# A vision tower with routed experts: GpSimd's wait for a scatter, and the place of a one-hot table

## The chip, the cores and the metric

The kernel runs on one core of one Trainium2 chip. The metric is device time in microseconds (us), the median of several executions. Before the change it was 946.81 us (three runs, 944.99 to 950.73).

## The reference, cut to what matters

The input is 32 images of 3 x 128 x 128. A tokenizer makes 64 tokens of 192 features of each, then follow a feed-forward layer, windowed attention and another feed-forward layer, a class token is put ahead (65 tokens an image, 2080 rows), then attention that keeps the 26 largest scores, and last the part that the change touches, a mixture of 128 experts:

```
topk_idx = top_k(sigmoid(x @ Wg.T) + e_bias, 6)      # 6 of 128 experts for each of 2080 rows
xb   = x[token_buf].reshape(E, CAP, H)               # up to 192 rows for each expert
gu   = einsum('ech,ehf->ecf', xb, W_gate_up);  g, u = split(gu, 2)
yb   = einsum('eci,eih->ech', silu(g) * u, W_down) * w_buf
out  = h + zeros.at[token_buf].add(yb) + silu(x @ Wsg) * (x @ Wsu) @ Wsd
```

Only experts that some row chose need work; with these inputs the experts' loop makes 20 rounds.

## The kernel before, in words

Five engines run programs of their own and meet at semaphores. Up to the experts the work goes over 16 tiles of 128 tokens; tables of words (`ORDER`) set by hand in which order each engine takes the pieces of neighbouring tiles. The normalized rows go to `x_rows` in DRAM, and what is not of the routed experts to `out`. The change touches none of these tables.

Then comes the experts' loop, `Fori(0, n2)`, each pass of which is two rounds (s = 0 and 1), one for each expert, on buffers that alternate. What a round v does:

- **SP** loads an expert's weights, two rounds ahead.
- **PE** makes the up products of half 0 (L996, L1001), then the index products (`slots_of`, L927) of expert v+2, which wait for `hot_ready`; then the up products of half 1, the transposes of the gathered rows of expert v+1 (L935), and the down products (L1012) of half 0 and, when DVE has them, of half 1.
- **ACT** makes the tanh of each half (L1191), copies the transposed rows (L1121), and scales the result into `y` (L1196, `y_done`).
- **DVE** finishes half 0 (L1628, L1632), waits for `add_done`, keeps the scatter's indices and weights (L1636, L1637), turns PE's index products into indices (L1551 to L1557, `index_ready`), then reads the number of the expert v+3 from a list (L1537, a register load) and builds a one-hot table of which row has which slot: a small part of 6 tiles (L1541, 1152 wide), after half 1 (L1628, L1632) a large part of 11 tiles (L1541, 2112 wide), and a copy of the weights (L1544), which signals `hot_ready`.
- **GpSimd** (POOL) issues the two gathers of expert v+2 once their indices are there (L1758), then waits for `y_done`, issues the two scatters that add y to `out` in DRAM (L1788), waits until they have landed (L1790), and signals `add_done`.

Indices that stand for no row point at dummy rows from T = 2080 on, of `x_rows` and of `out`. SP zeroes these with two transfers at the end of its first loads (L610, L611).

Of the kernel before, what the change touches and what calls it, by code (L numbers as in the profile page):

```python
# [6 lines left out]
D = 192  # L7
NP = (IMG // PATCH) ** 2
NKEY = NP + 1
T = B * NKEY  # L10
# [24 lines left out]
ROWS = T + CAP  # L35
# [271 lines left out]
def every(*stages):  # L307
# [4 lines left out]
SEMAPHORES = """  # L312
    h3_kept0 h3_kept1 xT_kept0 xT_kept1 fetched0 fetched1 at0_T at1_T at0_aT at1_aT zero_rows x_stored
    acc_stored0 acc_stored1 patch_mm xm_ready acc_ready c_xm_ready cls_x_stored  cls_acc_stored list_ready
# [16 lines left out]
def tower_kernel(nc, a, out):  # L331
# [4 lines left out]
    with ctx:  # L336
# [60 lines left out]
        zrows = sb("zrows", [CAP // 2, 2 * DX])  # L397
# [141 lines left out]
        def S(name):  # L539
            return named[name]  # L540
# [61 lines left out]
        def _(sp):  # L602
            sp.dma_start(xp[:], a["xp"][0]).then_inc(xp_loaded, 16)
            for group, done in ((patch_loads, loads_patch), (tokenizer_loads, loads_tokenizer),
# [3 lines left out]
                for dst, src in group:  # L608
                    sp.dma_start(dst, src).then_inc(done, 16)
            sp.dma_start(x_rows[T:ROWS, :].rearrange("(p r) d -> p (r d)", r=2), zrows[:]).then_inc(S("zero_rows"), 16)  # L610
            sp.dma_start(out[T:ROWS, :].rearrange("(p r) d -> p (r d)", r=2), zrows[:, 0:2 * D]).then_inc(S("zero_rows"), 16)  # L611

# [588 lines left out]
        def _(dve):  # L1201
# [419 lines left out]
            with dve.Fori(0, n2) as i:  # L1621
                for s in range(2):
                    v = 2 * i + s + 1
                    slots = slots_of(2 * i + s + 3, 1 - s)
                    for r in range(2):
# [8 lines left out]
                        if r == 0:  # L1634
# [4 lines left out]
                            indices_of(s, v + 2)  # L1639
                        if r == 0:  # L1640
                            next(slots)
                    run(slots)
# [3 lines left out]
        def _(pool):  # L1646
            G = nc.gpsimd
# [113 lines left out]
            def gathers():  # L1761
                yield "gather0"
                pool.wait_ge(S("x_stored"), 64 * TILES + 64)
                pool.wait_ge(S("cls_x_stored"), 32)
                pool.wait_ge(S("zero_rows"), 32)
                gather(0, 1)
                yield "gather1"
                gather(1, 2)

            pool.wait_ge(S("pe_ready"), 1)  # L1770
            pool.wait_ge(loads_tokenizer, 16 * len(tokenizer_loads))
# [4 lines left out]
            n2 = pool.value_load(lists[0:1, 2 * LIST:2 * LIST + 1], min_val=1, max_val=E // 2)  # L1776
            pool.sem_inc(S("add_done"), 2)
            for s in range(2):
                pool.wait_ge(S(f"acc_stored{s}"), 16 * TILES)
            pool.wait_ge(S("cls_acc_stored"), 16)  # L1780
            with pool.Fori(0, n2) as i:
                for s in range(2):
                    v = 2 * i + s + 1
                    gather(s, v + 2)
                    hold(pool, S("y_done"), v + 2)

                    for h in range(2):
                        G.indirect_dma_start(out[:, :], bass.IndirectOffsetOnAxis(add_index[s][:, h:h + 1], 0),  # L1788
                                             y[s][:, h, :], None, compute_op=ALU.add).then_inc(S("added"), 16)
                    pool.wait_ge(S("added"), 64 * i + 32 * s + 32)  # L1790
                    pool.sem_inc(S("add_done"), 1)
            for s in range(2):
# [78 lines left out]
```

## Time and profile before

| | us |
|---|---|
| median of three runs | 946.81 |
| the profiled execution, its own time | 954.78 |
| its span, first to last instruction | 953.0 |
| PE busy | 846.6 (89%) |
| DVE busy | 750.6 (79%) |
| ACT busy | 343.4 (36%) |
| POOL busy | 308.2 (32%) |

The profile cuts the span into 40 slices, lists who waited for whom, follows the chain of work that ended last back from the end, and gives each engine's instructions in order of time. The tiles take the first 700 us, the experts' loop the last 220. TensorE's granted clock was 0.965 over the whole, 0.97 in the loop. DMA engines are busy for about half of the loop's time.

### The profile page before, as it was taken

The page shows a single profiled execution, that of the slowest core. Times are in us where ns is not written, and L with a number is a line of the kernel's source. Part 1 is how long each engine was busy: PE and PEld are TensorE (multiplying, and loading weights), DVE is VectorE, ACT ScalarE, POOL GpSimd, SP SyncE. Part 2 cuts the span into 40 slices and gives each one's busy share as a digit, 9 for nine tenths or more (in the row PEclk, how much of TensorE's full clock was granted, in tenths as well). Part 3 has the DMA queues.
Part 4 walks back from the last instruction along what each step waited for, and adds up shares of the span by engine and source line. Part 5 has one row for each costly group of instructions (what it writes and reads, how often), then busy time and mean ns, then how long its engine had stood idle before and what let it go on. Part 6 is the DMA issues. An engine that isn't in the chain of part 4 may idle for free.

```text
span 953.0 us, 22207 instructions
## 1 busy us (share of the span) xinstructions
PE 846.6 (89%) x7603; PEld 766.5 (80%) x7603; DVE 750.6 (79%) x3738; ACT 343.4 (36%) x971; POOL 308.2 (32%) x350
## 2 busy tenths in 40 slices
PE   1787899899899899899899999998999999999993
PEld 1676688788798788788799999988878878878782
DVE  4256899999899899899999896988635666676662
ACT  0325554553553554544544435331100222122220
POOL 6021212412412312312313311031102556656564
PEclk8799999999999999999999999999986999999997
DMA  7410010110001001001101000001104455565541
GB/s 204 127 51 1 2 35 16 37 32 21 29 20 33 29 17 35 30 17 35 29 19 35 26 20 27 25 25 41 45 5 112 115 143 147 128 152 142 128 115 29
DMA packets 48663, 54.25 MB, mean 57 GB/s; under 512 B 8981, under 2 KB 41595, under 8 KB 48540
## 3 DMA queue, kind: packets, MB, share of 16 engines
q1 hardware_dynamic: 39372, 44.23, 16.3%
q0 software_dynamic: 6592, 7.28, 4.8%
q10 hardware_dynamic: 2608, 1.60, 0.7%
q8 instruction: 48, 0.79, 0.3%
q14 instruction: 43, 0.35, 0.1%
HBM read 42.40 MB, written 10.69 MB: 56 GB/s over the span
## 4 chain that ended last, share of the span: by engine, by line
DVE 41%; PE 28%; issue 11%; POOL 7%; DMA 7%; ACT 3%; SPq 2%; DVEq 0%; POOLq 0%; ACTq 0%
DVE b_arena L1497 10%; POOL b_arena L1758 4%; DMA out_rows<-b_hid,b_add_index 3%; POOL out_rows L1788 3%; DMA out_rows<-b_inner,b_add_index 3%; DVE b_top_a L1483 3%; PE p_big L685 3%; PE p_big L686 2%; DVE b_top_d L1483 2%; PE p_shared L830 2%; DVE b_top_c L1483 2%; PE p_shared L831 2%; DVE b_top_b L1483 2%; DVE b_rstd L1235 2%; PE p_small L866 2%
## 5 line engine op out<-in xcount | busy, mean ns | idle before, releaser
L1758 POOL DMA_INDIRECT b_arena<-x_rows,b_index x44 | 75.0, 1705 | 103.4 <-issue 66.3
L1541 DVE TENSOR_TENSOR b_arena<-b_iota_b,b_slot 128x1152 bf16<-128x1152 bf16 (+1 forms) x46 | 85.2, 1855 | 15.0 <-issue 15.0
L685 PE MATMUL p_big<-b_xT,b_ff1a 128*128 128x128 f32 x384 | 77.7, 285 | 1.4 <-ACT b_xT L1025 1.4
L686 PE MATMUL p_big<-b_xT,b_ff1b 128*128 128x128 f32 x384 | 76.9, 283 | 0.0
L1692 POOL TENSOR_TENSOR b_arena<-b_kY,b_mask_k 64x256 f32<-64x256 f32 x16 | 9.8, 611 | 204.8 <-ACT b_kY L1050 204.8
L1025 ACT COPY b_xT<-p_small 128x256 f32<-128x256 f32 (+1 forms) x97 | 35.5, 377 | 83.2 <-PE p_small L676 83.1
L1723 POOL TENSOR_TENSOR b_arena<-b_arena 128x768 f32<-128x768 f32 x16 | 27.0, 1690 | 117.6 <-DVE b_arena L1509 117.6
L685 PEld LDWEIGHTS p_big<-b_xT,b_ff1a 128*128 128x128 f32 x384 | 61.8, 200 | 2.5 <-ACT b_xT L1025 2.5
L686 PEld LDWEIGHTS p_big<-b_xT,b_ff1b 128*128 128x128 f32 x384 | 61.1, 200 | 0.0
L996 PE MATMUL p_big<-b_xeT,b_arena 128*116 128x192 f32 x320 | 60.1, 331 | 0.0
L719 PE MATMUL p_big<-b_arena,b_q_blk 128*128 128x256 f32 (+3 forms) x256 | 48.9, 334 | 12.4 <-ACT b_q_blk L1057 12.4
L719 PEld LDWEIGHTS p_big<-b_arena,b_q_blk 128*128 128x128 f32 x256 | 41.3, 190 | 19.3 <-POOL b_arena L1692 12.5
L996 PEld LDWEIGHTS p_big<-b_xeT,b_arena 128*116 128x116 f32 x320 | 51.5, 180 | 0.3 <-issue 0.3
L866 PE MATMUL p_small<-b_patch_w,b_xp 128*128 128x192 f32 x192 | 38.3, 353 | 11.8 <-DMA b_pe<-in_pe 9.9
L1107 ACT ACTIVATE b_th<-p_shared 116x256 f32<-116x256 f32 (+1 forms) x50 | 18.9, 377 | 71.5 <-PE p_shared L831 64.0
L866 PEld LDWEIGHTS p_small<-b_patch_w,b_xp 128*128 128x128 f32 x192 | 33.9, 205 | 13.2 <-issue 9.9
L1628 DVE SCALAR_TENSOR_TENSOR b_hid<-b_hid,p_big 116x384 f32<-116x384 f32 x20 | 11.1, 554 | 39.2 <-ACT b_hid L1191 39.2
L927 PEld LDWEIGHTS p_small<-b_rhs,b_arena 128*96 128x96 bf16 x748 | 37.0, 129 | 6.2 <-issue 4.7
L1497 DVE MATCH_REPLACE8 b_arena<-b_top_c,b_arena 128x65 f32<-128x65 f32 x208 | 41.7, 211 | 0.0
L836 PE MATMUL p_shared<-b_wsd,b_inner 116*128 116x192 f32 (+1 forms) x208 | 40.8, 354 | 0.9 <-DVE b_inner L1313 0.8
L1497 DVE MATCH_REPLACE8 b_arena<-b_top_b,b_arena 128x65 f32<-128x65 f32 x208 | 41.3, 211 | 0.0
L1497 DVE MATCH_REPLACE8 b_arena<-b_top_a,b_arena 128x65 f32<-128x65 f32 x208 | 41.1, 212 | 0.0
(367 smaller groups left out, 2589.6 us busy)
## 6 DMA issues: line engine op xcount, KB each, us to landing
b_arena<-in_w_gate_up SPq DMA_DIRECT2D x20, 464.0 KB
b_arena<-in_w_down SPq DMA_DIRECT2D x20, 336.0 KB
b_xp<-in_xp SPq DMA_DIRECT2D x16, 384.0 KB, 3.1
b_arena<-in_w_gate_up SPq DMA_DIRECT2D x40, 116.0 KB
xT_rows<-b_xmT SPq DMA_DIRECT2D x16, 128.0 KB, 1.8
b_xT_late<-xT_rows SPq DMA_DIRECT2D x16, 128.0 KB, 2.2
h_rows<-b_h SPq DMA_DIRECT2D x16, 96.0 KB, 1.6
x_rows<-b_xm SPq DMA_DIRECT2D x32, 48.0 KB, 2.0
```

The costliest lines, as they stand in the source:

```text
L685: mm(o, ff1a[:, c * 128:(c + 1) * 128], xTa[s][:], start=True, stop=False)
L686: last = mm(o, ff1b[:, c * 128:(c + 1) * 128], xTb[s][:], start=False, stop=True)
L719: last = mm(big[s][:, g, at:(4 + 2 * m) * keys], q_blk[s][:, m, g, :], k[:, g, :, :].rearrange("p j k -> p (j k)"), start=True, stop=True)
L836: last = mm(shared_bank(v, 4)[0:rows, 0:D], inner[:, c, 0:rows], wsd[:, c, :], start=(c == 0), stop=(c == NSC - 1))
L866: last = mm(small[2][:, 0:D], xp[:, c, :], patch_w[:, c, :], start=(c == 0), stop=(c == KC - 1))
L927: last = mm(lists_bank[s][0:HS, 400 + 6 * h:406 + 6 * h], hot[s][:, t, h * HS:(h + 1) * HS], rhs[s][:, t, :], start=(t == 0), stop=(t == N ...
L996: mm(big[r][0:SC, bank, j * CAP:(j + 1) * CAP], w_gu[s][:, c:c + SC], xeT[s][:, 0, :], start=(j == 0), stop=False)
L1025: cp((xT[s] if to is None else to)[:, 0:256].rearrange(both, t=128)[:, :, 0:rows], small[s][:, 0:256].rearrange(both, t=128)[:, :, 0:rows] ...
L1483: last = V.max(top[:, 8 * h:8 * h + 8], src[:, h * NKEY:(h + 1) * NKEY])
L1497: last = V.match_replace(work[:, h * NKEY:(h + 1) * NKEY], top[:, 8 * h:8 * h + 8], src[:, h * NKEY:(h + 1) * NKEY], -3e38)
L1541: last = tt(hot[s][:, tiles, :], iota_b[:, None, :].to_broadcast([128, n, CAP]), slot[:, tiles, bass.ds(e, 1)].to_broadcast([128, n, CAP]) ...
L1758: G.indirect_dma_start(xg[s][:, h, :], None, x_rows[:, :], bass.IndirectOffsetOnAxis(index[s][:, h:h + 1], 0)).then_inc(S(f"gathered{s}"), 16)
```

## The change

Three edits, with the bookkeeping of their semaphores:

1. GpSimd waits for a scatter's landing not behind its issue but just ahead of the next scatter's, and signals `add_done` there. `add_done` starts at 1 and not at 2, so DVE still reads it as "the scatter of round v-2 has landed".
2. DVE makes no part of the one-hot table between the halves. The register load, both parts and the copy stand behind half 1.
3. The two transfers of zero rows are issued by GpSimd behind its memsets. They count on the scatters' semaphore.

```diff
-            sp.dma_start(x_rows[T:ROWS, :].rearrange("(p r) d -> p (r d)", r=2), zrows[:]).then_inc(S("zero_rows"), 16)
-            sp.dma_start(out[T:ROWS, :].rearrange("(p r) d -> p (r d)", r=2), zrows[:, 0:2 * D]).then_inc(S("zero_rows"), 16)
...
                             indices_of(s, v + 2)
-                        if r == 0:
-                            next(slots)
                     run(slots)
...
-                pool.wait_ge(S("zero_rows"), 32)
+                pool.wait_ge(S("added"), 32)
                 gather(0, 1)
...
+            pool.wait_ge(presets, 1)
+            G.dma_start(x_rows[T:ROWS, :].rearrange("(p r) d -> p (r d)", r=2), zrows[:]).then_inc(S("added"), 16)
+            G.dma_start(out[T:ROWS, :].rearrange("(p r) d -> p (r d)", r=2), zrows[:, 0:2 * D]).then_inc(S("added"), 16)
             pool.wait_ge(S("pe_ready"), 1)
...
-            pool.sem_inc(S("add_done"), 2)
+            pool.sem_inc(S("add_done"), 1)
...
                     gather(s, v + 2)
                     hold(pool, S("y_done"), v + 2)
-
+                    hold(pool, S("added"), 64 * i + 32 * s + 32)
+                    pool.sem_inc(S("add_done"), 1)
                     for h in range(2):
                         G.indirect_dma_start(out[:, :], bass.IndirectOffsetOnAxis(add_index[s][:, h:h + 1], 0),
                                              y[s][:, h, :], None, compute_op=ALU.add).then_inc(S("added"), 16)
-                    pool.wait_ge(S("added"), 64 * i + 32 * s + 32)
-                    pool.sem_inc(S("add_done"), 1)
+            pool.wait_ge(S("added"), 64 * n2 + 32)
```

The order on DVE in a round of the loop, from the last index instruction to the end of the table, before (b_arena<-b_iota_b,b_slot is the one-hot table, b_rhs the copy of the weights; ISA rows are register work):

```order
1839 L1557 SCALAR_TENSOR_TENSOR b_index<-p_small,b_slot_a 96x2 [waits s_index_part]
1840 L1537 ISA
1841 L1537 TENSOR_LOAD b_lists
1842 L1537 ISA x2
1843 L1541 ISA
1844 L1541 TENSOR_TENSOR b_arena<-b_iota_b,b_slot 128x1152
1845 L1628 SCALAR_TENSOR_TENSOR b_inner<-b_inner,p_big 116x384 [waits s_eth1]
1846 L1632 TENSOR_TENSOR b_arena<-b_inner,p_big 116x384 [waits s_esilu]
1847 L1541 ISA
1848 L1541 TENSOR_TENSOR b_arena<-b_iota_b,b_slot 128x2112
1849 L1544 ISA
1850 L1544 COPY b_rhs<-b_wsplit 128x17x3
```

And with the change (its line numbers are lower by two):

```order
1839 L1555 SCALAR_TENSOR_TENSOR b_index<-p_small,b_slot_a 96x2 [waits s_index_part]
1840 L1626 SCALAR_TENSOR_TENSOR b_inner<-b_inner,p_big 116x384 [waits s_eth1]
1841 L1630 TENSOR_TENSOR b_arena<-b_inner,p_big 116x384 [waits s_esilu]
1842 L1535 ISA
1843 L1535 TENSOR_LOAD b_lists
1844 L1535 ISA x2
1845 L1539 ISA
1846 L1539 TENSOR_TENSOR b_arena<-b_iota_b,b_slot 128x1152
1847 L1539 ISA
1848 L1539 TENSOR_TENSOR b_arena<-b_iota_b,b_slot 128x2112
1849 L1542 ISA
1850 L1542 COPY b_rhs<-b_wsplit 128x17x3
```

The two instructions of half 1 moved ahead of the register load and of the small part.

On GpSimd, one round and the start of the next, before:

```order
277 L1758 DMA b_arena<-x_rows,b_index 96x256 [waits s_index_ready]
278 L1758 DMA b_arena<-x_rows,b_index 96x256
279 L1788 DMA out_rows<-b_hid,b_add_index 2272x192 [waits s_y_done]
280 L1788 DMA out_rows<-b_hid,b_add_index 2272x192
281 L1790 ISA
282 L544 REGISTER_ALU [waits s_added]
283 L1758 DMA b_arena<-x_rows,b_index 96x256 [waits s_index_ready]
```

And with the change:

```order
279 L1754 DMA b_arena<-x_rows,b_index 96x256 [waits s_index_ready]
280 L1754 DMA b_arena<-x_rows,b_index 96x256
281 L544 ISA [waits s_y_done]
282 L1788 DMA out_rows<-b_hid,b_add_index 2272x192 [waits s_added]
283 L1788 DMA out_rows<-b_hid,b_add_index 2272x192
284 L544 REGISTER_ALU
285 L1754 DMA b_arena<-x_rows,b_index 96x256 [waits s_index_ready]
```

The wait for the landed scatters no longer stands between a scatter and the next gather.

## Rows read from the trace of the kernel before

**Rows 1.** Chain of waits in the loop: start us, us, what.
```profile
791.88 3.39 DMA out_rows<-b_hid,b_add_index
795.46 0.79 issue
```

**Rows 2.** Timeline of one round, DVE, PE, ACT: start, us, instruction [idle before <-releaser].
```profile
784.89 0.55 DVE L1632 TENSOR_TENSOR b_arena<-b_inner,p_big 116x384 f32<-116x384 f32 x1
785.37 2.35 DVE L1541 TENSOR_TENSOR b_arena<-b_iota_b,b_slot 128x2112 bf16<-128x2112 bf16 x1
787.14 0.72 ACT L1196 ACTIVATE b_hid<-p_small,b_add_w 96x192 f32<-96x192 f32 x2 [3.00 <-PE p_small L1012]
787.63 0.19 DVE L1544 COPY b_rhs<-b_wsplit 128x51 bf16 x1
789.11 1.69 PE L927 MATMUL p_small<-b_rhs,b_arena 128*96 128x6 bf16 x34
790.88 0.23 DVE L1637 TENSOR_SCALAR b_add_w<-b_slot_w 96x2 f32<-96x2 f32 x1
791.71 0.16 DVE L1551 SCALAR_TENSOR_TENSOR b_slot_a<-p_small,b_dummy_f 96x2 f32<-96x2 f32 x1 [0.59 <-PE p_small L927]
792.23 0.16 DVE L1557 SCALAR_TENSOR_TENSOR b_index<-p_small,b_slot_a 96x2 int32<-96x2 f32 x1
792.97 0.55 PE L935 MATMUL p_small<-b_ident,b_arena 96*128 96x96 f32 x4
793.06 1.36 DVE L1541 TENSOR_TENSOR b_arena<-b_iota_b,b_slot 128x1152 bf16<-128x1152 bf16 x1 [0.67 <-issue]
793.25 0.49 ACT L1191 ACTIVATE b_inner<-p_big 116x384 f32<-116x384 f32 x1 [3.53 <-PE p_big L1001]
794.33 0.55 DVE L1628 SCALAR_TENSOR_TENSOR b_inner<-b_inner,p_big 116x384 f32<-116x384 f32 x1
794.91 0.55 DVE L1632 TENSOR_TENSOR b_arena<-b_inner,p_big 116x384 f32<-116x384 f32 x1
795.52 1.54 PE L1012 MATMUL p_shared<-b_arena 116*96 116x192 f32 x8 [0.70 <-DVE b_arena L1632]
```

**Rows 3.** Timeline of POOL in that round, and its last row of all.
```profile
786.29 2.26 POOL L1758 DMA_INDIRECT b_arena<-x_rows,b_index  x1 [2.99 <-issue]
788.86 0.95 POOL L1758 DMA_INDIRECT b_arena<-x_rows,b_index  x1 [0.30 <-issue]
790.11 1.46 POOL L1788 DMA_INDIRECT out_rows<-b_hid,b_add_index  x1 [0.30 <-issue]
791.88 1.43 POOL L1788 DMA_INDIRECT out_rows<-b_hid,b_add_index  x1 [0.30 <-issue]
...
942.06 1.44 POOL L1788 DMA_INDIRECT out_rows<-b_inner,b_add_index  x1 [0.30 <-issue]
```

**Rows 4.** The register load ahead of the table, by line: form, times, ns min/median/max, first and last start.
```profile
L1537 DVEq TENSOR_LOAD <-b_lists x2: 303/310/317, 782.3 to 792.3; - x2
```

**Rows 5.** Timeline of the first two rounds of the loop, DVE and POOL.
```profile
745.41 0.55 DVE L1632 TENSOR_TENSOR b_arena<-b_inner,p_big 116x384 f32<-116x384 f32 x1
751.14 1.44 POOL L1788 DMA_INDIRECT out_rows<-b_hid,b_add_index  x1 [0.30 <-issue]
751.68 0.15 DVE L1551 SCALAR_TENSOR_TENSOR b_slot_a<-p_small,b_dummy_f 96x2 f32<-96x2 f32 x1
754.88 0.55 DVE L1632 TENSOR_TENSOR b_arena<-b_inner,p_big 116x384 f32<-116x384 f32 x1
```

**Rows 6.** Timeline of the kernel's start: POOL, DVE and PE.
```profile
8.96 5.58 POOL L1660 MEMSET b_wsplit<- 128x6579 bf16 x1
21.50 0.35 DVE L1245 BATCH_NORM_STATS2 b_stat<-b_cls_row 32x6 f32<-32x192 f32 x1 [4.88 <-DMA b_eval_f<-in_evals]
30.65 0.48 PE L675 MATMUL p_small<-b_ident,b_h 128*128 128x128 f32 x1
```

**Rows 7.** DMA issues: out<-in, queue, times, KB each, us from issue to landing.
```profile
b_xp<-in_xp SPq DMA_DIRECT2D x16, 384.0 KB, 3.1
```

More of the change, by code:

```diff
@@ L312 @@
 SEMAPHORES = """
-    h3_kept0 h3_kept1 xT_kept0 xT_kept1 fetched0 fetched1 at0_T at1_T at0_aT at1_aT zero_rows x_stored
+    h3_kept0 h3_kept1 xT_kept0 xT_kept1 fetched0 fetched1 at0_T at1_T at0_aT at1_aT x_stored
     acc_stored0 acc_stored1 patch_mm xm_ready acc_ready c_xm_ready cls_x_stored  cls_acc_stored list_ready
```

## The prediction

> **What bounds the kernel now.** I read three views of the loop: the chain of waits, then the timeline of one round on every engine, then the same on GpSimd (POOL). The chain runs nearly all the way through GpSimd: scatter, 3.39 us until the scatter has landed, 0.79 us of issue, next gather [rows 1]. Read alone, it says that GpSimd's wait sets the beat and that its removal is worth over 3 us in a round. The timelines say otherwise. The beat is 10.02 us (DVE's L1632 of half 1 at 784.89 and 794.91) [rows 2], and the last scatter at 942.06 stands 15 rounds of 10.01 after the one at 791.88 [rows 3]. In that beat GpSimd's first gather takes 2.26 us and the second, just behind it, 0.95 [rows 3]. The first ends at 788.55, that is 0.83 after DVE's large table part has ended (785.37 + 2.35 = 787.72) [rows 2]: it is held while DVE builds the table. Without that hold GpSimd's circle would be about 10.0 - 1.3 = 8.7. It has room, and takes DVE's beat only because of the hold.
>
> The beat itself is a circle through PE, ACT and DVE. PE starts the index products at 789.11, ACT's tanh of half 1 starts at 793.25 and ends at 793.74, but DVE is then busy with the small table part (793.06 to 794.42), so its L1628 starts only at 794.33, L1632 at 794.91, and PE, which has stood still for 0.70, goes on at 795.52 [rows 2]. That 0.5 to 0.6 is what edit 2 goes for.
>
> **Edit 2, the table.** Without the small part in between, DVE takes half 1 as soon as the tanh ends. I take 0.06 for a hop (L1632 ends at 795.46, PE starts at 795.52 [rows 2]). From the start of PE's index products to the start of L1632: 793.25 - 789.11 = 4.14, tanh 0.49, hop 0.06, L1628 to L1632 0.58, sum 5.27 [rows 2].
>
> If nothing else were late, PE would start the next index products 4.22 after L1632 as now (784.89 to 789.11), and the beat would be 5.27 + 4.22 = 9.49. But those products need the table of this very round (`hot_ready`). Now the table is ready at 787.82 and PE wants it at 789.11, a slack of 1.3 us. The change eats more than that. Behind L1632 there now come:
> - the register load with its arithmetic. Between L1557's start and the small part's start stand 0.83 us, in which DVE is idle for 0.67 [rows 2]; the load, 0.31 long, begins at 792.3, 0.1 after L1557 has started [rows 4]. So the sequencer fetches ahead of a running instruction, but not past one that waits for a semaphore, and L1632 waits for one. I take 0.83 from the start of L1632, of which its own 0.55 cover the most;
> - the small part, 1.27 until the next instruction starts (793.06 to 794.33);
> - the large part, 2.26 (785.37 to 787.63);
> - the copy of the weights, 0.19, and the hop, 0.06.
>
> Sum 4.61 instead of 4.22 [rows 2]: PE gets the table 0.39 later than it wants it. **The new beat is 5.27 + 4.61 = 9.88**, 0.14 under 10.02; 0.39 of the 0.53 are handed back as a new wait, PE's L927 for DVE's L1544.
>
> How many beats: 20 rounds, 19 between the first and the last L1632. Now the first took 9.47 (745.41 to 754.88) [rows 5] and 18 took 10.01 (the rate of rows 3), together 189.7. With the change 19 x 9.88 = 187.7, that is -2.0. The first round also sheds about 0.2 of the small part's delay.
>
> The fast first beat bears the theory out. In it DVE's L1551 came 0.54 us after the second scatter had started; later it comes at 791.71, just behind the end of the first scatter (790.11 + 1.46 = 791.57), and L1637 lasts 0.23 [rows 2, 3, 5]. DVE's small operations are held there by GpSimd, the index is late by 0.5, so the small part is, and so is half 1. With the small part gone this hold has nothing to pass on: about 1.5 us lie between the index and half 1.
>
> **Edit 1, the wait.** GpSimd gets free 3 to 4 us earlier, which I cost at nothing for the beat, since PE, ACT and DVE cover it. What is queued behind the new wait: the two scatters and `add_done`. The scatter that is waited for has landed long before. DVE needs `add_done` at L1636, just ahead of L1637, which starts 6.0 us after L1632; GpSimd signals it once `y_done` has come (ACT's L1196 ends at 787.86, 3.0 after L1632 [rows 2]) and its own gathers are out. After this edit the gather starts when its index is there: index products + 3.28 (L1557's end, 792.39) + 0.79 of issue; then 0.95, 0.30, 0.95 [rows 1 to 3], which ends 6.27 after the index products, before the table parts for the most part. Then the scatters wait for y, are held by the large part (to 4.4 after L1632), and are out by 7.5. Now they are out at 793.31, 8.4 after L1632. At the end of the kernel that gap counts: **-0.9**. If instead the gather is caught by the table, it is +0.4.
>
> **Edit 3, the zero rows.** SP loses two issues ahead of the second tile's patches; PE takes these only behind the first tile's feed-forward layer, so an earlier load adds slack and no time. GpSimd's memsets end at 14.54; two transfers follow, each at most about a scatter's 1.46 [rows 3, 6]. They delay its first tile by up to 3 us, hidden, as PE reads that tile at 30.65, behind the class token's steps, and these begin when the loads up to b_eval_f have landed, at 21.50 [rows 6]. What can cost is DMA traffic ahead of that: 192 + 144 = 336 KB, nearly the 384 KB whose load lands in 3.1 us [rows 7]. So 0 to +2.7; SP issues these loads one by one and the DMA engines have gaps, so I take **+0.4**, near the lower end.
>
> **Sum.** -2.0 - 0.2 - 0.9 + 0.4 = -2.7 us on the profiled execution's 954.78 (span 953.0). That one stands 8 above the median of the runs; against the median 946.81 the same difference gives **944.1**.
>
> **A rule weighed.** The table part reads two tiles in SBUF, and the second gather would be out 6.27 us after the index products, while the table wants to start at 5.27 + 0.83 = 6.10: they meet by 0.17. In the rows, DVE's small part started at 793.06, its usual 0.83 behind L1557, while the second scatter ran to 793.31: not held. The Trainium skill (SBUF — State Buffer, "Who interferes with whom") says that a VectorE instruction with two SBUF inputs and a GpSimd instruction that reads SBUF exclude each other, that whoever issues first keeps the shared ports for the whole instruction, and that the other fully blocks. The held gather agrees with it (2.26 against 0.95), the 793.06 start does not. By the rule the table would wait for the gather, which is the second rival.
>
> **The rivals.**
> 1. *The table is in time* (chance 0.16): the load runs ahead of L1632, or PE's wish is later than I think; the beat is 9.49. 19 x 9.49 = 180.3, -9.4, and the other terms make -10.1: **936.7**. For it: PE's own circle allows it. Against: the load starts only behind the instruction that waits, in every round shown.
> 2. *Gather holds the table* (0.18): + 0.2 a beat (0.17 and a hop), 10.08: 191.5, +1.8, with the rest +1.1: **947.9**. For it: L1637 and L1551 look held by a scatter. Against: 793.06.
> 3. *GpSimd falls behind the table, slower* (0.08). GpSimd has four transfers (0.95, 0.95, 1.46, 1.43 and four gaps of 0.30: 6.0), the table now shuts it out for 3.7 in one stretch; together 9.7 of 9.88. If it slips until both gathers stand behind the table, the second is out at 0.83 + 3.53 + 0.83 + 0.30 + 0.95 = 6.4 after L1632, and PE's transposes (L935, 3.86 behind the index products [rows 2]) want the rows at 4.61 + 3.86 = 8.47. That leaves 2.0 for landing. Scatters take 1.96 from the end of issue (795.27 - 793.31); gathers now have 3.16 (789.81 to 792.97) without a wait seen. It decides from 2.0 on: 0 to 1.1 a beat; with 0.7 the beat is 10.58, +11.3 and, with +0.4 and -0.2 and +0.4, +11.9: **958.7**.
> 4. *The zero rows cost their full 2.7* (0.08): **946.4**.
> 5. *The chain is right and GpSimd's wait was the bound*: then the beat falls until PE's circle stops it, which is rival 1 or my 9.88, so it needs no time of its own.
>
> The forecast keeps 0.50. Two measurements of this kernel differ by up to about 1% (9.5 us) without meaning, which is what I call no change. Faster by more: rival 1, 0.16, and a little of the rest, 0.17. Slower by more: rival 3, and something for what I don't see, 0.09. No change 0.74. The range goes from rival 1 less a us, 935.5, to 951, above rival 2 with the zero rows' bound; rival 3 stays out.
>
> **What would show it.** In the profile after: L1632 to L1632 at 9.9 in the loop; DVE's L1541 small starts 0.8 behind L1632's start and the large part 1.3 behind that; PE's L927 shows a wait of about 0.4 for DVE's L1544, while its L1012 waits 0.1 to 0.2 instead of 0.70; GpSimd's gathers start 0.8 behind the index and take 0.95 both, its first scatter is held instead and lasts over 2; its last scatter comes about 1 us sooner behind the last L1632. The start: b_cls_row's first operation at 21.5 to 22. I am wrong if L927 waits for nothing (rival 1), if DVE's small part starts over 1.0 behind L1632 (rival 2), or if L935 waits for a gather (rival 3).

## The result, and the profile after

| | before | after |
|---|---|---|
| median of the runs, us | 946.29 (4 runs, 944.99 to 950.73) | 961.12 (4 runs, 956.01 to 963.98) |
| profiled execution, us | 954.78 | 956.01 |
| granted clock of TensorE, mean | 0.965 | 0.958 |

The ratio is 1.0142 (interval 1.0084 to 1.0201): slower by 1.4%, clear of the noise, where 944.1 and no change were forecast; whether by more than 2% the interval leaves open. The profiled executions, though, are only 1.2 us apart. Both facts need a cause, and they are two causes. The profiled execution of before, 954.78, is not one of the four timed ones, and it lies above them all.

The timeline of the changed kernel for two rounds (start, us, instruction, times; idle before it and its releaser in brackets), against [rows 2]:

```profile
783.65 0.56 DVE L1630 TENSOR_TENSOR b_arena<-b_inner,p_big 116x384 f32<-116x384 f32 x1
784.46 3.63 DVE L1539 TENSOR_TENSOR b_arena<-b_iota_b,b_slot 128x1152 bf16<-128x1152 bf16 x2 [0.26 <-issue]
788.00 0.19 DVE L1542 COPY b_rhs<-b_wsplit 128x51 bf16 x1
788.24 1.69 PE L925 MATMUL p_small<-b_rhs,b_arena 128*96 128x6 bf16 x34 [0.30 <-DVE b_rhs L1542]
789.79 1.54 PE L994 MATMUL p_big<-b_xeT,b_arena 128*116 128x192 f32 x8
791.26 0.91 PE L999 MATMUL p_big<-b_xeT,b_arena 64*116 64x192 f32 x8
793.33 0.55 DVE L1630 TENSOR_TENSOR b_arena<-b_inner,p_big 116x384 f32<-116x384 f32 x1
797.94 1.69 PE L925 MATMUL p_small<-b_rhs,b_arena 128*96 128x6 bf16 x34 [0.32 <-DVE b_rhs L1542]
799.49 2.62 PE L994 MATMUL p_big<-b_xeT,b_arena 128*116 128x192 f32 x8
802.04 1.47 PE L999 MATMUL p_big<-b_xeT,b_arena 64*116 64x192 f32 x8
804.66 0.55 DVE L1630 TENSOR_TENSOR b_arena<-b_inner,p_big 116x384 f32<-116x384 f32 x1
```

The beat is the time from one L1630 of half 1 to the next. The first round is the one that was forecast: small and large part in one stretch, a wait of 0.30 at L925, a beat of 9.68. The second has the same work and takes 11.33: the eight products of L994 need 2.62 instead of 1.54, those of L999 1.47 instead of 0.91. The windows of PE there (us, PE busy and its products, granted clock, DMA share, GB/s) say why:

```profile
797.00:799.00 2.00, 1.68 (x32) 1.00 0.53 165
799.00:800.00 1.00, 1.00 (x18) 0.89 0.37 19
800.00:801.00 1.00, 1.00 (x5) 0.50 0.41 55
801.00:802.00 1.00, 1.00 (x4) 0.50 0.62 55
802.00:803.00 1.00, 1.00 (x7) 0.50 0.35 64
803.00:804.00 1.00, 1.00 (x12) 0.90 0.17 53
```

The granted clock is 0.50 (1.2 GHz of 2.4) from just behind the index products until 803.2. It happens in 6 of the 19 rounds, every third, for 3.4 us each time: from 769.1, 799.8, 830.5, 861.2, 892.0 and 922.7. The trace of before has no fall between its first and last round (its 0.97 above is the mean with the stretches just ahead of and behind them):

```profile
746.00:936.00 190.00, 177.48 (x1636) 1.00 0.56 135
```

From the first L1630 to the last of the loop, the change takes 193.94 (743.23 to 937.17: 13 beats of 9.69 and 6 of 11.33), the trace of before 189.67.

On GpSimd (timeline), against [rows 3]:

```profile
787.72 1.70 POOL L1788 DMA_INDIRECT out_rows<-b_hid,b_add_index  x1 [3.68 <-issue]
789.73 1.44 POOL L1788 DMA_INDIRECT out_rows<-b_hid,b_add_index  x1 [0.30 <-issue]
791.49 0.96 POOL L1754 DMA_INDIRECT b_arena<-x_rows,b_index  x1 [0.32 <-issue]
792.75 0.95 POOL L1754 DMA_INDIRECT b_arena<-x_rows,b_index  x1 [0.30 <-issue]
...
943.25 1.44 POOL L1788 DMA_INDIRECT out_rows<-b_inner,b_add_index  x1 [0.30 <-issue]
```

The gathers are no longer held, the last scatter starts 6.08 behind the last L1630 (6.98 before), and the chain that ended last now has next to nothing of GpSimd and its DMA in it (7% and 7% before):

```profile
DVE 45%; PE 39%; issue 6%; ACT 4%; SPq 2%; DVEq 2%; POOL 0%; DMA 0%; ACTq 0%; POOLq 0%
```

The start, against [rows 6]:

```profile
14.50 0.70 POOL L1767 DMA_DIRECT2D x_rows<-b_zrows  x1
15.19 0.58 POOL L1768 DMA_DIRECT2D out_rows<-b_zrows  x1
22.41 0.35 DVE L1243 BATCH_NORM_STATS2 b_stat<-b_cls_row 32x6 f32<-32x192 f32 x1 [4.95 <-DMA b_eval_f<-in_evals]
```

### The profile page after: what moved, and what is told of

The parts are those of the page before. It is cut to its first block, busy times and chain, and to the rows that moved or that the text cites. A ratio compares the mean times of both kernels' runs of the same rounds, so it can differ in the third digit from the quotient of the medians.

```text
span 954.2 us, 22228 instructions
## 1 busy us (share of the span) xinstructions
PE 854.9 (90%) x7603; PEld 771.7 (81%) x7603; DVE 750.2 (79%) x3738; ACT 345.3 (36%) x971; POOL 284.9 (30%) x352
## 4 chain that ended last, share of the span: by engine, by line
DVE 45%; PE 39%; issue 6%; ACT 4%; SPq 2%; DVEq 2%; POOL 0%; DMA 0%; ACTq 0%; POOLq 0%
DVE b_arena L1495 9%; DVE b_arena L1539 5%; PE p_small L925 4%; PE p_big L994 4%; DVE b_top_a L1481 3%; PE p_shared L828 3%; PE p_big L683 2%; PE p_shared L829 2%; PE p_big L684 2%; PE p_big L999 2%; PE p_shared L834 2%; DVE b_top_d L1481 2%; DVE b_top_c L1481 2%; PE p_small L690 2%; DVE b_top_b L1481 2%
## 5 line engine op out<-in xcount | busy, mean ns | idle before, releaser
L994 PE MATMUL p_big<-b_xeT,b_arena 128*116 128x192 f32 x320 | 66.5, 355 | 0.0
L1754 POOL DMA_INDIRECT b_arena<-x_rows,b_index x44 | 45.1, 1025 | 54.4 <-issue 42.3
L994 PEld LDWEIGHTS p_big<-b_xeT,b_arena 128*116 128x116 f32 x320 | 56.4, 194 | 0.4 <-issue 0.3
L1626 DVE SCALAR_TENSOR_TENSOR b_inner<-b_inner,p_big 116x384 f32<-116x384 f32 x20 | 11.1, 554 | 51.4 <-ACT b_inner L1189 51.4
L864 PE MATMUL p_small<-b_patch_w,b_xp 128*128 128x192 f32 x192 | 37.9, 351 | 12.1 <-DMA b_pe<-in_pe 10.3
L925 PEld LDWEIGHTS p_small<-b_rhs,b_arena 128*96 128x96 bf16 x748 | 36.7, 128 | 13.4 <-DVE b_rhs L1542 13.2
L925 PE MATMUL p_small<-b_rhs,b_arena 128*96 128x6 bf16 x748 | 38.6, 187 | 7.3 <-DVE b_rhs L1542 7.3
L1788 POOL DMA_INDIRECT out_rows<-b_inner,b_add_index x20 | 31.8, 1588 | 44.6 <-issue 44.6
L1788 POOL DMA_INDIRECT out_rows<-b_hid,b_add_index x20 | 31.5, 1576 | 44.6 <-issue 44.6
L864 PEld LDWEIGHTS p_small<-b_patch_w,b_xp 128*128 128x128 f32 x192 | 33.7, 204 | 13.5 <-issue 10.3
```

What stands on the lines that cost most here:

```text
L864: last = mm(small[2][:, 0:D], xp[:, c, :], patch_w[:, c, :], start=(c == 0), stop=(c == KC - 1))
L925: last = mm(lists_bank[s][0:HS, 400 + 6 * h:406 + 6 * h], hot[s][:, t, h * HS:(h + 1) * HS], rhs[s][:, t, :], start=(t == 0), stop=(t == N ...
L994: mm(big[r][0:SC, bank, j * CAP:(j + 1) * CAP], w_gu[s][:, c:c + SC], xeT[s][:, 0, :], start=(j == 0), stop=False)
L1754: G.indirect_dma_start(xg[s][:, h, :], None, x_rows[:, :], bass.IndirectOffsetOnAxis(index[s][:, h:h + 1], 0)).then_inc(S(f"gathered{s}"), 16)
```

## The experiments

The kernels ran in groups, each group with runs of the kernel before beside it; those of e1 to e18 are each on one chip, seven chips in all. The groups differ: before took 946.3 beside the change and beside e9 to e12, 955.5 beside e1 to e4, 955.65 beside e5 to e8, and later 955.3 (e13 to e15), 955.4 (e16), 960.1 (e17) and 954.6 (e18). So ratios go by their own group, and what happens in the loop is read from each trace. "Loop" is the time from the first to the last multiplication that makes `einner` of half 1 (20 of them, 19 beats). For before's own trace it is 189.67, a first beat of 9.47 and 18 of 10.0.

| kernel | median us | ratio (interval) | loop | beats | clock falls |
|---|---|---|---|---|---|
| the change | 961.12 | 1.0142 (1.0084, 1.0201) | 193.94 | 9.69, 11.33 | 6 |
| e1 edits 1 and 3 | 942.6 | 0.9857 (0.9831, 0.9883) | 179.88 | 9.46 | 0 |
| e2 edit 2 | 962.45 | 1.0065 (1.004, 1.009) | 196.35 | 9.69, 10.3 to 12.0 | 2 |
| e3 edit 3 | 956.62 | 1.0003 (0.9982, 1.0025) | 189.66 | 10.0 | 0 |
| e4 load ahead | 941.75 | 0.985 (0.9822, 0.9877) | 177.42 | 9.34 | 0 |
| e5 edit 2, load ahead | 961.11 | 1.0061 (1.0033, 1.0089) | 194.21 | 9.34, 9.9 to 11.5 | 0 |
| e6 four fillers | 955.87 | 1.002 (1.0001, 1.004) | 190.5 | 10.02 | 0 |
| e7 e4, table later | 945.28 | 0.9908 (0.9876, 0.994) | 180.75 | 9.51 | 0 |
| e8 change, table later | 959.98 | 1.0054 (1.0032, 1.0076) | 193.97 | 9.87, 11.50 | 4 |
| e9 change again | 958.91 | 1.0147 (1.0094, 1.02) | 193.95 | 9.69, 11.33 | 6 |
| e10 e4, half 1 later | 946.35 | 0.9995 (0.9976, 1.0013) | 182.0 | 9.58 | 0 |
| e11 one filler | 949.19 | 1.0026 (1.0008, 1.0045) | 184.1 | 9.69 | 0 |
| e12 two fillers | 948.54 | 1.0039 (1.0016, 1.0062) | 184.15 | 9.69 | 0 |
| e13 before | 953.69 | 0.999 (0.9972, 1.0007) | 189.12 | 9.47 x2, 10.0 | 0 |
| e14 as e1 | 944.69 | 0.9889 (0.9848, 0.993) | 179.92 | 9.46 | 0 |
| e15 as e4 | 942.28 | 0.9852 (0.9815, 0.9889) | 177.41 | 9.34 | 0 |
| e16 before | 955.84 | 0.9998 (0.9978, 1.0017) | 189.1 | 9.47 x2, 10.0 | 0 |
| e17 before | 960.88 | 1.0012 (1.0001, 1.0023) | 193.98 | 9.46, 10.8 to 11.6 by turns | 0 |
| e18 change | 958.44 | 1.0049 (1.0031, 1.0068) | 193.96 | 9.69, 11.33 | 6 |

### Taking the change apart: e1, e2, e3

e1 is the change with the small part back between the halves:

```diff
                             indices_of(s, v + 2)
+                        if r == 0:
+                            next(slots)
```

> Edits 1 and 3 without edit 2: the small part of the table stands between the halves as before. Theory A (edit 2 costs the time: its wait for the table makes TensorE's granted clock fall once in three rounds): no wait ahead of PE's index products, the clock stays at 1.00 from the first to the last round. And since the scatter no longer runs while DVE's L1637 works, the small part comes 0.5 us earlier and is over when the tanh of half 1 ends: a beat of 9.5 us instead of 10.0, so 19 beats of about 9.5 = 180, some 9 to 11 us faster than before (0.989). Theory B (edit 1 costs it, by transfers that meet in the DMA queues, or edit 3 by a later start): this run is as slow as the whole change, 1.014.

e2 is before without those two lines. e3 is before with the zero rows issued by GpSimd, on their own semaphore:

```diff
-            sp.dma_start(x_rows[T:ROWS, :].rearrange("(p r) d -> p (r d)", r=2), zrows[:]).then_inc(S("zero_rows"), 16)
-            sp.dma_start(out[T:ROWS, :].rearrange("(p r) d -> p (r d)", r=2), zrows[:, 0:2 * D]).then_inc(S("zero_rows"), 16)
...
+            pool.wait_ge(presets, 1)
+            G.dma_start(x_rows[T:ROWS, :].rearrange("(p r) d -> p (r d)", r=2), zrows[:]).then_inc(S("zero_rows"), 16)
+            G.dma_start(out[T:ROWS, :].rearrange("(p r) d -> p (r d)", r=2), zrows[:, 0:2 * D]).then_inc(S("zero_rows"), 16)
```

> Edit 2 alone: the wait for the scatter stands where it was. Theory A: the beat is 9.7 to 9.9 us where the clock holds, PE's index products wait 0.3 us or more for the table, and the clock falls in several rounds, 1.6 us each; 1.00 to 1.02 of before. GpSimd, whose scatters are still waited for, may be late for y or for add_done on top of it, since the table shuts it out for longer in one stretch: up to 10.1 a beat. Theory B: the beat stays at 10.0 or falls, with a clock of 1.00 all through: 1.00 or less.

> Edit 3 alone: the zero rows by GpSimd, on a semaphore of their own. Theory A: nothing in the loop, and 0 to 1 us at the start: 1.000 to 1.001. Theory B in its second form (the start is what costs): 1.01, with the first tile's transposes (L675) a few us later than 30.65.

e1 is faster than before by 12.9 us: 9.8 of them are in the loop (179.88 for 189.67); the rest is not assigned. e2 is slower. Edit 3 costs nothing that its interval (0.9982 to 1.0025, about 2 us either way) could show. The timeline of e2 shows the same wait at the index products, and one on DVE behind it:

```profile
784.18 1.69 PE L927 MATMUL p_small<-b_rhs,b_arena 128*96 128x6 bf16 x34 [0.31 <-DVE b_rhs L1544]
787.19 0.15 DVE L1551 SCALAR_TENSOR_TENSOR b_slot_a<-p_small,b_dummy_f 96x2 f32<-96x2 f32 x1 [1.46 <-PE p_small L927]
```

L1551 comes 3.0 us behind the start of the index products, where the change has it 1.7 behind (788.24 to 789.97). GpSimd issues a scatter at that time (786.42 to 787.88), as it does where L1551 is late in [rows 2, 3]; that the scatter holds it is inferred from this meeting. The table in one stretch pays only beside edit 1.

e2 also shows something that I overlooked: PE waits 0.30 to 0.35 ahead of its index products in all 19 rounds, as in the change, with beats of 9.69 among them, up to three in a row, and yet the clock falls only in the first and the fourth round. After that (windows of PE in e2):

```profile
790.00:945.00 155.00, 141.71 (x1298) 1.00 0.54 130
```

So that wait alone does not make a fall. Something else has a part in it, such as the times at which the rounds come.

### Taking the wait away: e4, e5

e4 is the change with the register load moved ahead of half 1, where DVE is idle; e5 is edit 2 with the load ahead, on top of before, without edits 1 and 3.

```diff
-            def slots_of(j, s):
+            def slots_of(j, s, ahead=False):
...
+                if ahead:
+                    yield
...
-                    slots = slots_of(2 * i + s + 3, 1 - s)
+                    slots = slots_of(2 * i + s + 3, 1 - s, ahead=True)
...
                             indices_of(s, v + 2)
+                            next(slots)
```

> The whole change, but the register load of the table stands ahead of half 1, where DVE is idle anyway, and only the two parts and the copy behind half 1. Theory A: the table is ready 0.27 us earlier, so the wait of PE's index products (0.3 us) falls to below 0.1, the beat to 9.4 to 9.5. If the wait is what makes the clock fall, it holds at 1.00 and the loop takes 19 x 9.45 = 180, 10 us less than before: 0.99. If the clock falls whatever the wait (because of the beat itself), some rounds still take 11 us and the ratio is 1.00 to 1.01.

> The table behind half 1 with its register load ahead of half 1, as in e4, but GpSimd waits for its scatter right behind it, as before, and SP writes the zero rows. It asks what edit 1 is good for. GpSimd's circle: four transfers and their gaps 6.0, the landing and issue 4.2 behind the second scatter's start, less its 1.4 that is in the 6.0, and 3.7 in which the table shuts it out, of which at least the gathers' part counts: 9.7 to 11. Theory A (with the table in one stretch GpSimd's old wait becomes the bound): the beat is over 9.34 and uneven, some rounds with PE's L935 waiting for a gather's landing as in e2, ratio 0.99 to 1.01. Theory C (edit 1 does nothing, the load alone gives the 15 us): beat 9.34, ratio 0.985.

The table starts 0.47 behind L1632's start, not 0.81, and PE's index products wait for nothing (timeline of e4; its first row, GpSimd's second gather, counts further down):

```profile
786.57 0.96 POOL L1757 DMA_INDIRECT b_arena<-x_rows,b_index  x1 [0.30 <-issue]
786.84 0.55 DVE L1632 TENSOR_TENSOR b_arena<-b_inner,p_big 116x384 f32<-116x384 f32 x1
787.31 3.62 DVE L1541 TENSOR_TENSOR b_arena<-b_iota_b,b_slot 128x1152 bf16<-128x1152 bf16 x2
790.85 0.19 DVE L1544 COPY b_rhs<-b_wsplit 128x51 bf16 x1
791.09 1.69 PE L925 MATMUL p_small<-b_rhs,b_arena 128*96 128x6 bf16 x34
```

In the windows, PE is busy in all of 745 to 925, at full clock:

```profile
745.00:925.00 180.00, 180.00 (x1669) 1.00 0.63 143
```

A table that starts 0.34 us sooner gives 16.5 us of loop. The shorter beat is 19 x 0.35 = 6.7 of it; the other 9.8 are the six falls. e5 says again that edit 2 without edit 1 loses: no fall, but beats of up to 11.5.

### Filling the wait: e6, e11, e12

Products that nobody reads, put ahead of the index products (4 in e6, 1 in e11, 2 in e12):

```diff
                         if r == 0:
+                            for n in range(4):
+                                mm(lists_bank[s][0:96, 412:508], w_gu[s][:, 96 * n:96 * n + 96], xeT[s][:, 0, 0:96],
+                                   start=True, stop=True)
                             slots_of(s, v + 2)
```

> The whole change, and ahead of PE's index products four products of 96 columns that nobody reads, 0.3 to 0.5 us, in the time in which PE waits for the table. Theory A1 (the clock falls because PE does little around the index products): the beat stays at 9.7 to 9.8, the granted clock is 1.00 in all 19 beats, the loop takes 185 and not 194, ratio 0.995. Theory A2 (the beat itself, or the index products alone, makes it fall): the clock still falls in every third round, 6 times 1.6 us, ratio 1.005 or more.

> The change with one idle-time product of 96 columns (0.23 of PE's time in two passes) ahead of the index products; four of them made all falls vanish but lengthened the beat to 10.02. Here the table still sets the beat, 9.69, and the wait is 0.1 to 0.15. Theory A (idle time next to the index products): fewer falls than the change's 6, or none; ratio 0.993 with none. Rival A2 (it is the beat of 9.69 and the order of work that do it, not the idle time): 6 falls as before, ratio 1.01.

> The same with two such products (0.46): PE's wait of 0.30 is filled nearly whole, the beat still 9.69 to 9.75. Theory A: no falls, ratio 0.993 to 0.996. Rival A2: falls in every third round, ratio 1.01. If this one has none and the one with one product has some, the size of the idle time decides.

e6 had no fall either, but four products are more than the wait, and its beat is 10.02. e11 and the change make the cleanest pair of the study. e11 has the same beat as the change, 9.69 in all 19 rounds, the same work on every other engine, and PE is not idle ahead of L925 (timeline of e11; L1004 is the filler; last, PE's window over the loop):

```profile
790.35 0.91 PE L999 MATMUL p_big<-b_xeT,b_arena 64*116 64x192 f32 x8
791.19 0.41 PE L1004 MATMUL p_small<-b_xeT,b_arena 128*96 128x96 f32 x2
791.57 1.69 PE L925 MATMUL p_small<-b_rhs,b_arena 128*96 128x6 bf16 x34
793.12 1.54 PE L994 MATMUL p_big<-b_xeT,b_arena 128*116 128x192 f32 x8
749.00:932.00 183.00, 183.00 (x1668) 1.00 0.60 140
```

No fall, and a loop of 184.1 beside e9's 193.95 on the same chip; the medians are 9.7 us apart. So the falls cost 9.8 us, and with the 0.3 us of idle time filled they are gone; the filling changes nothing else that the traces show, as the table still sets the beat. I had expected a rest of the wait in e11, but one product covers it, so e12 adds nothing. The ratios I gave (0.993) were wrong, since before took 946 here and not 955; the second cause, below.

### Moving the wait: e7, e8, e10

Two memsets of 128x104 on DVE between the table and the copy to `rhs` (e7 on e4, e8 on the change):

```diff
                     if tiles.stop == NT:
+                        if not isinstance(j, int):
+                            for x in (top_a, top_b)[:2]:
+                                V.memset(x[:], 0.0)
```

And in e10 (on e4) a memset of 128x400 between the two instructions of half 1:

```diff
+                        if r == 1:
+                            V.memset(sq0[:, 0:400], 0.0)
                         dve.wait_ge(S("esilu"), 2 * v - 1 + r)
```

> e4 (table behind half 1, its load ahead, GpSimd's wait moved) with two small fills of tiles that are free here, 0.2 to 0.3 us, on DVE ahead of the copy that signals the table. So the wait of the whole change comes back by another cause, with a beat of 9.4 to 9.6 in place of 9.69. Theory A: PE's index products wait 0.1 to 0.2 us; the clock falls in some rounds once the wait is as long as in the whole change, in none if it is near 0. Any beat with a fall is 1.6 us longer. If the register load as such were the cause, nothing falls here and the ratio is 0.986.

> The whole change with the same two fills: the wait ahead of PE's index products is 0.5 to 0.6 us and not 0.3, the beat without falls 9.9 to 10.0. Theory A: the clock falls at least as often as in the whole change, so the loop takes 19 x 9.95 + 6 x 1.6 or more, 199 or more, ratio 1.02. If the falls came from a beat of 9.69 that happens to keep step with something periodic, there are fewer of them, and the ratio is 1.00 to 1.01.

> The version with the register load ahead of half 1 (beat 9.34, no fall of the clock), with 0.4 of extra work (a memset of 128x400) on DVE between L1628 and L1632 of half 1. It makes PE wait too, but mostly ahead of the down products of half 1 (0.25, the slack there was 0.15) and only some 0.1 ahead of the index products; the beat would be 9.7, as the change's. Theory A by place (the wait must stand next to the index products, whose 34 products have 6 columns each): no or hardly a fall of the clock, 9.7 in all rounds, ratio 0.993. Rival A2 (any idle time of that size in a round of that length does it): falls in about every third round as in the change, beats of 11.3 among them, ratio 1.01.

e7: a gap of 0.14 ahead of L925 (the products of L999 end at 787.43, L925 starts at 787.57), no fall. e8: the wait is 0.48 instead of 0.30, but the falls are fewer, 4 and not 6, and the ratio is 1.0054. Theory A asked for as many or more and for 1.02; what came is what I had written down for the rival, a beat that happens to keep step with something periodic:

```profile
791.86 1.69 PE L925 MATMUL p_small<-b_rhs,b_arena 128*96 128x6 bf16 x34 [0.48 <-DVE b_rhs L1545]
```

The falls in e8, 3.4 us long again, start at 782.1, 823.0, 864.0 and 915.2, that is in beats 4, 8, 12 and 17 of the 19. So, as in e2, the length of the wait does not fix how often the clock falls; when the rounds come may be the other part, and no run varied that alone. The beat cannot be the whole cause either, since e11 and e12 have the change's beat and no fall: at that beat the falls need the idle time. e10 moved the wait as meant (timeline):

```profile
788.61 1.54 PE L1010 MATMUL p_small<-b_arena 116*96 116x192 f32 x8 [0.23 <-DVE b_arena L1634]
```

0.23 ahead of the down products in every round, beats of 9.58, no fall. With before's 0.70 at the same place [rows 2] and up to 2.23 in e17, also without a fall, it says that idle time there did no harm at these beats. It is weaker evidence on the place than e11 is on the idle time, since neither beat nor size is the change's.

### The other 10 us: e9, e13 to e18

All without a new edit: the change (e9, e18), the kernel before (e13, e16, e17), e1 and e4 again (e14, e15).

> The change as it was timed, once more beside the three kernels below. Theory A (PE's wait of 0.3 ahead of the index products makes TensorE's clock fall in some rounds): ratio 1.01 +- 0.006, beats of 9.69, and some (4 to 7 of 19) of 11.3 with a granted clock of 0.50 just behind the index products. Rival (the slow rounds were a mishap of the first trace): all beats 9.69 and a ratio near 0.993.

> The kernel before, unchanged, to have a second trace of it beside runs of the same group. Its median was 946.3 in two groups of runs (the first, and that of e9 to e12) and 955.5 in two others (e1 to e4, e5 to e8), while the change took 959 to 961 in both kinds and its loop of 193.9 us explains only +4.3 over the traced loop of before (189.67). Theory P: before has two forms of its loop, the traced one with beats of 10.02, where DVE's small operations are held by a scatter, and one with the beat of its first round, 9.47; a run near 946 has a loop of 19 x 9.47 = 180, near 955 one of 190. Rival Q (the difference lies ahead of the loop, in the tiles): the loop is 189.7 in both, and the start of the loop is 9 us sooner in a run near 946.

> Edits 1 and 3 without edit 2, once more. Theory P: beats of 9.46 again, about 942.6; where before takes 946 the ratio is 0.996, where it takes 955.5 it is 0.986. Rival Q (edits or chip move the tiles): beats 9.46, but 933, that is 0.986 whatever before takes.

> The change with the register load ahead of half 1, once more. Theory P: beats of 9.34, about 941.8; ratio 0.995 where before takes 946, 0.985 where it takes 955.5. Rival Q: 932 where before takes 946, 0.985 in both cases.

> The kernel before, unchanged, for a trace from a group of runs in which it takes 946 rather than 955. Theory P: where it takes 946, its loop keeps the beat of 9.47 of its first rounds and is about 180 long. Rival Q: its loop is 189.7 there too, with beats of 10.0, and the loop starts 9 us sooner. If this group takes 955, the trace has beats of 10.0 again and tells nothing new.

> The kernel before, unchanged, for a trace from a group of runs in which it takes 946. All kernels tried so far take 764.3 to 766 us outside their loops (median less the loop's length in the trace), on every group; if that holds here, a run of 946 has a loop of 180, 19 beats of 9.47 (theory P). Rival Q: a loop of 189 and 757 outside it. If this group takes 955, beats of 10.0 again.

> The change a third time. Both groups that it ran in so far had the kernel before at 946; there the ratio was 1.014 and 1.0147. Theory P (the change has one form of its loop, 193.9, everywhere, and the kernel before has several: 9.47 kept, 10.0, and 9.46 with 10.8 by turns): the change takes 959 to 961 here too; where before takes 955 the ratio is 1.004 to 1.006, where it takes 960 it is 1.000, where it takes 946 1.014 again. Rival Q (the groups differ ahead of the loop, for every kernel alike): 968 to 974 and the ratio 1.014 again, whatever before takes.

The change is the same in all three groups that it ran in: three traces, six falls at every third round, loop 193.94 to 193.96, medians 958.4 to 961.1. The kernel before is not. e13 and e16 begin with two beats of 9.47 and go over to 10.0; e17 goes over to 9.46 and 10.8 to 11.6 by turns and takes 960.9. On its timelines (start, us; the table's large part stands between GpSimd's rows) one sees the first gather either just ahead of the large table part, so that the second is held, or caught by it, and then DVE's L1551 late:

```profile
800.30 0.96 POOL L1758 DMA_INDIRECT b_arena<-x_rows,b_index  x1 [2.74 <-DMA out_rows<-b_hid,b_add_index]
800.40 2.35 DVE L1541 TENSOR_TENSOR b_arena<-b_iota_b,b_slot 128x2112 bf16<-128x2112 bf16 x1
801.56 2.01 POOL L1758 DMA_INDIRECT b_arena<-x_rows,b_index  x1 [0.30 <-issue]
809.86 2.35 DVE L1541 TENSOR_TENSOR b_arena<-b_iota_b,b_slot 128x2112 bf16<-128x2112 bf16 x1
810.13 2.91 POOL L1758 DMA_INDIRECT b_arena<-x_rows,b_index  x1 [3.04 <-issue]
813.35 0.96 POOL L1758 DMA_INDIRECT b_arena<-x_rows,b_index  x1 [0.30 <-issue]
```
```profile
806.20 0.16 DVE L1551 SCALAR_TENSOR_TENSOR b_slot_a<-p_small,b_dummy_f 96x2 f32<-96x2 f32 x1
816.99 0.16 DVE L1551 SCALAR_TENSOR_TENSOR b_slot_a<-p_small,b_dummy_f 96x2 f32<-96x2 f32 x1 [1.37 <-remote]
```

So the loop of before has several forms, and what chooses one was not settled (I take it for small differences in when a scatter has landed; no run varied that). Outside the loop little differs: the median less the loop is 762.7 to 767.2 in all 19 rows of the table, whatever the group (e18: 958.44 - 193.96 = 764.5; e17: 766.9), and a profiled execution's own time less its loop 762.1 to 769.1. For before at 946.3 this leaves a loop of 179.1 to 183.6, and its first beats kept throughout would make 19 x 9.47 = 179.9. The four kernels traced on the very chip where before took 946.26 (e9 to e12) narrow it: 764.3 to 765.1 outside the loop, so 181.2 to 182.0 for before, not 189.7. Nor is it the clock: executions of before with the same mean granted clock of 0.964 took 946.1 to 947.7 beside e9 and 954.6 to 954.7 beside e13. No trace of before was taken in a group where it takes 946, so this form is inferred, not shown. What is shown is its consequence: in e18, beside a before of 954.64, the change costs 1.0049 and not 1.014, as written down ahead of it (958.44, for 959 to 961), and rival Q (the groups differ ahead of the loop) would have had the change at 968 to 974.

## Why the prediction was wrong

- **Edit 2, the circle of half 1**: right and a little better than forecast. The beat without a fall is 9.69, not 9.88. The table starts 0.81 behind L1630 (forecast 0.83), the parts take 3.6, the wait at L925 is 0.30 to 0.32 (0.39). From L1630 to the next index products it is 4.59 (4.61). L1630 comes 5.09 behind the index products and not 5.27, since the tanh starts 3.98 behind them (792.22) and not 4.14, and DVE 0.03 behind the tanh; why was not looked into. So rival 1's 9.49 is 9.34 in e4. PE's down products (L1010) wait for nothing, where 0.1 to 0.2 was forecast.
- **The step that failed: "0.39 of the 0.53 are handed back as a new wait".** The wait was priced at its length. It costs more by the clock: six rounds are longer by 1.64 each (11.33 - 9.69), 9.8 us. The sum has no term for the clock, and all rivals, too, kept the granted clock of the loop as it was. e11 shows it by filling the wait at an unchanged beat, e4 by taking away its cause. That there are six falls and not two or none stays open (e2, e8).
- **The second failure: the base.** The sum was made against a profiled execution of 954.78, and its -2.7 was then set on a median of 946.81, with the remark that the one stands 8 above the other, and differences of up to 1% were taken to be without meaning. But 946, 955 and 960 come back as the medians of whole groups. They were most likely not the same form of the kernel: the traced one had the beat of 10.02, and the median, as inferred above, one near the 9.47 of its own first beat [rows 5]. Against that form the change is 19 x (9.69 - 9.47) = +4.2, falls +9.8, tail -0.9: +13.1. Measured were +14.8 (961.12 - 946.29) and, in e9, +12.65. Against the traced form it is 193.96 - 189.67 - 0.9 = +3.4; measured in e18 +3.8.
- **Edit 1**: costed at nothing for the beat. That was wrong: e5 and e4 differ by edits 1 and 3 only, and their loops are 194.21 and 177.42. Alone with edit 3 it gives 9.46 in all rounds but the first and the best price of the three edits. The table still holds both gathers there, as in no round of the change (timeline of e1):

```profile
800.84 2.00 POOL L1756 DMA_INDIRECT b_arena<-x_rows,b_index  x1 [0.54 <-issue]
803.14 3.02 POOL L1756 DMA_INDIRECT b_arena<-x_rows,b_index  x1 [0.30 <-issue]
```

  What is gone is the late L1551 (its counterpart L1549 starts 2.05 behind the index products in every such round, 806.73 to 808.78, and 2.60 in [rows 2]). Tail -0.9: measured 6.98 - 6.08 = 0.9.
- **The held gathers**: right. The first starts 0.85 behind the index's end (forecast 0.79) and 0.32 behind the last scatter, the second 0.30 behind it, and both take 0.95; the first scatter is held instead, but 1.70 to 1.74 long and not over 2.
- **Edit 3**: +0.4 forecast; e3 has 1.0003 with about 2 us either way, which cannot tell 0.4 from nothing. The class token's first operation came at 22.41 instead of 21.50 in this trace.
- **The rivals**: "the table is in time" did not come true in the change, but e4 makes it true and gives 9.34. "Gather holds the table" did not come about: the second gather stands at 792.75 to 793.70 and the table starts at 794.15, its usual 0.82 behind L1630, so they never met and the change does not test the rule. e4 does: its second gather runs from 786.57 to 787.53 and takes its usual 0.96, and the table starts at 787.31, right behind L1632. In e17 the large part starts 0.10 behind a gather (800.30 and 800.40), and both keep their usual length. A gather that was first did not hold the table, so the rule that the prediction weighed does not hold here on the table's side, as its 793.06 had said. "GpSimd falls behind, slower" had the sign and nearly the time (958.7), but not the place: no transposes (L933) waited for a gather in the change. In e2, without edit 1, they did:

```profile
L935 PE MATMUL p_small<-b_ident,b_arena 96*128 96x96 f32 x76 | 10.4, 260 | 1.6 <-DMA b_arena<-x_rows,b_index 1.6
```

  (by line: busy, mean ns of one, idle before it and its releaser.)

**The best version** is e4: all three edits and the register load ahead of half 1. e1, edits 1 and 3 alone, is nearly as good: 0.9 us behind in the group of both, 2.4 behind in the second (944.69 and 942.28), with ranges that overlap both times, though the loops (179.9 and 177.4) differ each time. The medians of e4 and e15, the same kernel, 941.75 and 942.28, are under every median of both kernels, 0.985 of before in groups where that takes 955.5. It was not run where before takes 946; from 764.3 + 177.4 I would expect 942 there too, or 0.995.

## What to carry to other kernels

Don't price a new idle time of TensorE at its length alone: read the granted clock round by round in the next trace, and if it falls behind the idle time, fill that or remove its cause. When the profiled execution is further from the median than the runs are from each other, don't add a difference worked out on one to the other; look in the trace for a beat that changes (here 9.47 in the first round, 10.0 later), since the timed runs may keep the form that the trace leaves. And a loop in which one engine's transfers and another's table get in each other's way can have several beats (here 9.47, 10.0 and 9.46 with 10.8 to 11.6); with edits 1 and 3 the beat was 9.46 on both chips that e1 and e14 ran on.

## What the runs showed of the hardware

- The granted clock fell to 0.50 (1.2 GHz) for 3.4 us although PE was idle for only 0.30 us of each 9.69, ahead of 34 products of 6 columns each; it did not fall with 0.70 idle in each 10.02 at another place (before), nor with 0.23 in 9.58 (e10), nor with 0.14 ahead of the same products in 9.51 (e7); and with 0.31 there in e2 it fell twice in 19 rounds. The pattern (every third round) was the same in three traces, of which at least two are from different chips (10 and 15). What exactly decides was not settled. The Trainium skill (TensorE: Matmul & The Clock Gate, Part 1) says that the gate goes by how busy PE has been of late. e11 agrees with it: busy in the gap, the clock stays at 1.00.
- What a fall costs stands in two rows: the eight products of L994 take 2.62 for 1.54, those of L999 1.47 for 0.91, together 1.64, which is the whole of 11.33 - 9.69.
- DVE's table part with two inputs in SBUF started while GpSimd issued a scatter (793.06 against an end at 793.31 [rows 2, 3]), a large part started 0.10 behind a gather and took its usual 2.35 (e17), a small part started 0.22 before a gather's end (e4), and gathers were held by the table (2.91 in e17, 2.00 and 3.02 in e1, for 0.95). So in these rows only GpSimd's issue is ever held, and the table is not, even where it comes second. Which beat before takes (9.47, 10.0, or 9.46 with 10.8 to 11.6) goes with where the gathers meet the table; that this chooses it is inferred.
